# A mixture-of-experts layer whose second matrices move from token-major fp32 products to stationary float32r halves with 512 gated tokens moving

## The reference

```python
logits = x @ Wg + bg
topk_vals, topk_idx = top_k(logits, 2);  topk_w = softmax(topk_vals)
h = relu(einsum('bsd,edf->bsef', x, W1) + b1)
eo = einsum('bsef,efd->bsed', h, W2) + b2
mixed = sum(take(eo, topk_idx) * topk_w)
y = mixed + x
out = layernorm(gamma * (y - mu) * rsqrt(var + eps) + beta)
```

## Time and profile before

| | us |
|---|---|
| median of 3 runs (lowest, highest) | 232.52 (230.89, 234.33) |
| span of the profiled execution | 229.2 |
| its own time | not given apart; the runs' median is 3.3 above the span |
| PE busy | 215.3 (94%) |
| DVE busy | 181.3 (79%) |
| ACT busy | 142.5 (62%) |
| POOL busy | 111.6 (49%) |

### The profile page before, as it was taken

The page is one execution under the profiler, slowest core; times in us unless marked ns, Lnnn a source line. Parts: engine busy times, 40 slices in busy tenths (PEclk is TensorE's granted clock), DMA queues, the critical chain, the costliest instruction groups (busy, mean ns, idle before and its releaser), DMA issues.

```text
span 229.2 us, 7210 instructions
## 1 busy us (share of the span) xinstructions
PE 215.3 (94%) x2724; PEld 184.4 (80%) x2724; DVE 181.3 (79%) x622; ACT 142.5 (62%) x248; POOL 111.6 (49%) x219
## 2 busy tenths in 40 slices
PE   8989899999999989999999999999999999999970
PEld 7766677778777667778887999789988999889970
DVE  0589998999899899776755779897798868875885
ACT  2488899999999995674489300991029610596112
POOL 5089889999889995513630400252002600040484
PEclk9999999999999999999999999999999999999996
DMA  5951534765569941000000000001000100001001
GB/s 149 286 124 34 106 61 51 171 133 119 138 125 156 156 90 19 14 3 1 3 0 0 3 0 1 0 3 46 4 0 0 46 3 1 0 4 46 1 16 34
DMA packets 32455, 12.32 MB, mean 54 GB/s; under 512 B 19907, under 2 KB 32291, under 8 KB 32419
## 3 DMA queue, kind: packets, MB, share of 16 engines
q1 hardware_dynamic: 31554, 11.48, 24.5%
q10 hardware_dynamic: 864, 0.36, 0.6%
HBM read 6.33 MB, written 1.05 MB: 32 GB/s over the span
## 4 chain that ended last, share of the span: by engine, by line
PE 81%; DVE 6%; DMA 5%; ACT 3%; issue 2%; SPq 1%; DVEq 0%; ACTq 0%
PE bank L1326 13%; PE scoreT_pair L1326 12%; PE score_pair L1298 11%; PE scoreT_pair L1298 8%; PE bank L1042 6%; PE bank L1046 5%; DMA qT_all<-mT 5%; PE bank L965 4%; PE scoreT_pair L997 4%; PE bank L1003 3%; PE score_pair L981 3%; PE scoreT_pair L945 2%; PE bank L1059 2%; ACT early L737 2%; PE bank L940 1%
## 5 line engine op out<-in xcount | busy, mean ns | idle before, releaser
L1383 DVE TENSOR_REDUCE rowmax<-score_pair 128x8 f32<-128x1024 f32 x32 | 39.0, 1218 | 3.3 <-PE score_pair L981 2.0
L608 POOL TENSOR_TENSOR ve<-mv,table 128x4 f32<-128x4 f32 (+1 forms) x12 | 3.3, 277 | 78.1 <-DVE mv L1743 60.2
L737 ACT ACTIVATE early<-scoreT_pair 128x1024 f32<-128x1024 f32 x32 | 32.9, 1027 | 6.0 <-PE scoreT_pair L997 5.9
L1326 PE MATMUL bank<-w,early 128*128 128x128 f32 x256 | 30.1, 276 | 0.0
L1326 PE MATMUL scoreT_pair<-w,early 128*128 128x128 f32 x256 | 29.9, 275 | 0.0
L1326 PEld LDWEIGHTS bank<-w,early 128*128 128x128 f32 x256 | 29.5, 192 | 0.3
L1326 PEld LDWEIGHTS scoreT_pair<-w,early 128*128 128x128 f32 x256 | 29.2, 192 | 0.0
L1298 PE MATMUL score_pair<-x2T_part,w_part 128*128 128x512 f32 x108 | 28.4, 397 | 0.0
L880 ACT ACTIVATE early<-score_pair,b 128x512 f32<-128x512 f32 x38 | 26.0, 691 | 3.2 <-PE score_pair L1298 2.6
L1042 PE MATMUL bank<-early,v_pad 128*32 128x128 f32 x512 | 26.5, 279 | 0.4 <-DVE attnT L1399 0.3
L1046 PE MATMUL bank<-early,head_ones 128*32 128x128 f32 x512 | 25.8, 273 | 0.0
(11 more groups left out here) (229 smaller groups left out, 474.0 us busy)
## 6 DMA issues: line engine op xcount, KB each, us to landing
w<-in_w SPq DMA_DIRECT2D x8, 256.0 KB, 3.8
x_ext<-in_x SPq DMA_DIRECT2D x4, 256.0 KB, 5.4
qT_all<-mT SPq DMA_DIRECT2D x32, 32.0 KB, 2.3
early<-in_xT SPq DMA_DIRECT2D x3, 256.0 KB, 4.5
early<-in_ctxT SPq DMA_DIRECT2D x3, 256.0 KB, 5.1
out<-qkv_all SPq DMA_DIRECT2D x3, 256.0 KB, 2.3
table<-in_tables SPq DMA_DIRECT2D x1, 321.0 KB
qT_all<-stack SPq DMA_TRANSPOSE x13, 3.4
```

Source lines behind the costliest of these rows:

```text
L737: act.activation(prob[n % 2][:, 2 * u:2 * u + 2, :, :], scoreT_pair[:, :].rearrange("p (i j s) -> p i j s", i=2, j=QUAD), ACT.Exp, scale=S ...
L1326: mm = pe.matmul(expert_bank[k % 4][:, e4 * D:(e4 + 1) * D], hT[:, f, n * P:(n + 1) * P], w2[:, f, :], start=(c == 0), stop=(c == CH - 1))
L1383: dve.tensor_reduce(rowmax[:, H // 2 * u:H // 2 * (u + 1)], score_pair[:, :].rearrange("p (r t) -> p r t", t=S), AX_X, ALU.max).then_inc(s ...
```

## The change

1. **The second layer by feature.** For all but six (group, expert) pairs, `second(k)` on PE holds a 128 x 128 piece of w2 stationary and moves 512 tokens. w2 and the activations are split into float32r parts: w2_high x high, w2_low x high, w2_high x low, three matmuls of 512 columns a chunk. All chunks of a group add up in one bank (`yT_bank`), feature-major.
2. **The gate goes in ahead of the product.** DVE's `gated` takes the bank of the first layer: max(h, -b1) times the gate, in one instruction of 512 columns. (The relu leaves out +b1, which the b2 product makes up: b1 through w2 is added to b2 for each expert, by 16 matmuls, `turn_b1`, that take the place of idle ones, and by `shift_b2` on DVE.) ACT's `highs` rounds the result to float32r, POOL's `low` (for indices 2 and 3 of a group DVE's) subtracts for the low part. Buffers: 3 gated, 5 high, 4 low. `second` runs four chunks behind `hidden` (LAG).
3. **The gate as rows.** To multiply by token along the free axis, the gate must lie across all partitions: gates are transposed on PE, copied by ACT (`gate_rows`), written to DRAM and read back from there, spread over 128 partitions, 256 KB for each expert and group, all on the SP queue (`spread_gates`).
4. **The way back.** `keep_yT` on ACT copies the bank, `y_back` on PE transposes it in four pieces, `y_add` on DVE adds it to `acc`, one group late (in g3 at once).
5. **By token as before** stay experts 0 to 3 of g0, and 6 and 7 of g3.
6. **Other moves.** The first layer's banks are three in rotation instead of four. `pre_rows` and `post_results` go from DVE to ACT. The work of the next and of the last group is laid between the `gated` instructions on DVE. w2 is split by ACT and POOL in the correlation; POOL's `spread_b1` (a memset of 1536 columns and 17 small instructions) stands ahead of the inverse deviation of row tile 14.

```diff
+BY_TOKEN = ((0, 1, 2, 3), (), (), (6, 7))
+LAG = 4
+N_GATED, N_HIGH, N_LOW = 3, 5, 4
+LOW_ON_DVE = (2, 3)
...
         def hidden_bank(g, c):
-            return later_bank[c] if g else bank[c % 4]
+            return bank[(NCH * g + c) % 3]
+        yT_bank = (bank[4], bank[3], bank[4], bank[3])
...
+            def spread_gates(g):
+                wait_later(sp, "gate_rows_ready", g + 1)
+                sp.dma_start(gate_dram[g].rearrange("n e t -> (n e) t"), gate_rows[:, :]).then_inc(s["gate_kept"], 16)
+                wait_later(sp, "gate_kept", 16 * (g + 1))
+                for e in range(E):
+                    if e in BY_TOKEN[g]:
+                        continue
...
+                    sp.dma_start(gate_wide[e].rearrange("p (n t) -> p n t", n=GT), gate_dram[g, :, e, :].partition_broadcast(P))\
+                        .then_inc(s_gate[e][0], 16)
...
+            def low(g, i):
...
+                pool.tensor_tensor(low_in[k % N_LOW], gated_in[k % N_GATED][:, :], high_in[k % N_HIGH][:, :].bitcast(F32), ALU.subtract)\
+                    .then_inc(s["low_pool"], 1)
...
             def body(g):
-                hidden(g, 0, NCH)
+                highs(g, 0, 2)
+                rows(g + 1)
+                highs(g, 2, 4)
                 pre(g + 1)
+                highs(g, 4, 5)
+                keep_yT(g - 1)
+                highs(g, 5, 8)
                 exp_gap(g + 1)
+                highs(g, 8, 12)
                 gateT_copy(g + 1)
+                highs(g, 12, 15)
+                results(g - 1)
+                highs(g, 15, 16)
...
+                for i, (w, x) in enumerate(((w2_high, high_in[k % N_HIGH][:, :]), (w2_low, high_in[k % N_HIGH][:, :]), (w2_high, low_in[k % N_LOW]))):
+                    if i == 2:
+                        wait_low(pe, k)
+                    mm = pe.matmul(yT_bank[g][:, :], w[:, c, :], x, start=(k == first and i == 0), stop=(k == last and i == 2),
+                                   skip_group_check=True)
...
+            def layers(g, first, end):
+                for c in range(first, end):
+                    hidden(g, c, c + 1)
+                    second(gated_no(g, c) - LAG)
...
+            layers(3, 6, 12)
+            for c in range(12, NCH):
+                hidden(3, c, c + 1)
+                second(gated_before(G) - LAG + c - 12)
+            experts(3, 0)
+            experts(3, 1)
+            y_back(3)
+            experts(3, 2)
+            experts(3, 3)
...
+                    dve.scalar_tensor_tensor(gated_in[k % N_GATED][:, :], hidden_bank(g, c)[:, :], b1_neg[:, c:c + 1], gate_wide[e], ALU.max, ALU.mult)\
+                        .then_inc(s["gated"], 1)
```

More of the change, by code:

```diff
@@ new lines, in layers, with body @@
+            def layers(g, first, end):
+                for c in range(first, end):
+                    hidden(g, c, c + 1)
+                    second(gated_no(g, c) - LAG)
+            def body(g):
+                layers(g, 0, 1)
+                b2_mix(g)
+                layers(g, 1, 4)
+                x2_transpose(g + 1)
+                layers(g, 4, 6)
+                logits(g + 1)
+                y_back(g - 1)
+                layers(g, 6, 12)
+                gate_transpose(g + 1)
+                layers(g, 12, NCH)
@@ L1743, in gather, with sums_statistics, post_rows @@
                 dve.bn_aggr(mv3[:, n, :], st3[:, n, :]).then_inc(s["y3_aggr"], 1)
-            def post_sums(g, call, tiles=ALL):
-                numbers = range(tiles.start, tiles.stop)
-                for n in numbers:
+            def sums_statistics(g):
+                wait_later(dve, "y_added", g + 1)
+                statistics(lambda n: acc[:, g, n, :], st3, "y3_stats", mv3, "y3_aggr", g)
+            def post_rows(g):
+                for n in range(GT):
                     dve.wait_ge(s["y3_aggr"], GT * g + n + 1)
```

640 lines of the change are left out of this document (468 added, 172 removed).

## The result

The changed kernel takes 279.12 us (276.12 to 279.88, four runs) against 231.94 (230.89 to 234.33) for the kernel before in the same comparison: 1.200 times as long, 95% interval 1.194 to 1.207. The forecast said slower, but 244.5 us, and its range ended at 255. Of the 47.2 us that came, 12 were foreseen. The profiled execution has a span of 277.8 us, 48.6 above that of before. (Each run's time is some 2 us above its own span.

A forecast was written before the change was run, and what follows sets the result against it. PE alone was taken to bound the experts, POOL's chain the end. Span 227.3 plus 10.9 of waits plus 3.0 for the port gave 241.2, 12.0 above 229.2; 232.5 + 12.0 = 244.5 us, range 232 to 255.

The forecast's parts named there:

- my sum: Whole kernel: span 227.3 + 10.9 of PE's waits + 3.0 for the shared port = 241.2, 12.0 above 229.2.
- Part 1, PE's work: PE in g0 to g3: 11.1 us less from 52 chunks by feature, transposes added, net 8.9 us less.
- Part 2, the end: POOL's chain after g3: starts 1.2 us earlier, runs 1.0 shorter, `spread_b1` adds 0.3; span 227.3 if PE never waits.
- Part 3, what PE now waits for: g0 to g3: PE waits for DVE, gates and x2 rows, as three engines are nearly full; 10.9 us.
- Gates for g1: Start of g1: gate rows' write and spread read in series delay `gated`, 1.3 us (0 to 4).
- the end of g3: PE's waits at the end of the last group, 0.5 us.
- Part 4, POOL against DVE: g0 to g3: DVE instructions with two SBUF operands are held until POOL's ends, 3.0 us (0 to 12).
- My bounds for this part: Shared port: nothing where POOL happens to wait for DVE, up to 1.27 us for each place; 0 to 12 in all.
- The rival: Shared port costs much more: about 15 places lose half of POOL's 1.27 and more, 9 us, time 250; chance 0.12.
- what was to show it right: g1 25 to 28 us, PE waiting for `gated`, pairs 1.36, g0 ending on DVE, gates' DMA wait, POOL near 225, held DVE.
- POOL's start: End: POOL starts on the last group's tile 0 near 225, the last result 12.2 us after.
- what was to show it wrong: POOL on tile 0 before 216, `second` matmuls not 0.227, or PE waiting most for ACT or the DMA queue.

The follow-up runs named there:

- experiment 2: Changed kernel with each POOL low replaced by a same-size subtraction on constant tensors that nothing waits for, low part left out of the result: 275.96 us.
- experiment 1: Changed kernel without POOL's low subtractions; PE's third matmul moves the high part instead, except in the two chunks a group that DVE splits: 255.2 us.
- experiment 8: Changed kernel without POOL's lows, with spread gates read early from g0's rows and ACT's result rows and DVE's means moved later in the last group: 247.72 us.
- experiment 4: Kernel before, with POOL running one unused 512-column subtraction for each chunk of g1 and g2: 245.97 us, 1.055 times the kernel before.
- experiment 3: Changed kernel with each of POOL's low subtractions split into two of 256 columns: 273.31 us.
- experiment 5: Changed kernel with 18 (g1) and 26 (g2) extra small matmuls into a free bank where PE waited: 277.20 us.

## Why the prediction was wrong

The sign and its reason were right: an 8.9 us cut of PE's work is worth almost nothing, since the end is POOL's chain and the engines around PE were to become late. The size was off by 35 us. The steps from run to run share it out (medians, each good to about 2 us):

- *Lock by the lows*, experiment 2 less 1: 20.8 us, of which up to 2.8 may be waits in POOL's queue.
- *Waits for the lows*, the changed kernel less experiment 2: 3.1.
- *Gates and the order at the end*, experiment 1 less 8: 7.5 (3.1 and 4.1 alone, in the kernel with lows).
- *Experiment 8 over the kernel before*: 15.9, of which 7.7 were in my sum (12.0 less 3.0 for the port and 1.3 for the gates), 2.3 are the chunk pair and up to 4.4 the lock in g0 and ahead of it.

That the four add up to 47.3 for the 47.2 measured proves nothing, since each begins where the one ahead ends. What can be tested is inside them: the 19.6 us of longer instructions beside the 20.8, the 7.2 of two separate runs beside the 7.5, and 14.4 named of the 15.9. Some 1.5 us stay open.

By the steps of the prediction:

**Part 1, PE's work:** right in kind. Where the two layers alternate, a float32r matmul takes 0.233, not 0.227. The earlier trace rows has 1.39 and 1.36 for six matmuls, and I took the lower one as the rate for all 342.

**Part 2, the end:** right: 12.2 us from POOL's start to the last result, measured 12.2. The front: I gave `spread_b1` 0.3 us. It costs nothing; but from the last softmax reciprocal to the first layer's first whole chunk it is 17.39 us (101.53 to 118.92) where it was 16.06 (99.07 to 115.13), in experiments 1 and 8 17.4 and in experiment 4, whose front is the old one, 16.06. The 1.33 us are x2's first two rows, 1.93 instead of 0.60, held beside POOL's additions of the cross bias (114.19 to 116.69), which now come behind w2's low half. That is a part of the lock that no low causes.

**Part 3, what PE waits for, 10.9 us:** in experiment 8, where only these are left, it is 27.6 us from the transposes for g2's x2 (153.67) to those for g3's (181.25), beside 27.2 in the sum (23.9 + 2.3 + 1.0). Two items were too small. Gates for g1, 1.3 (0 to 4): the read took 5.4 us in g1 (5.9 in the median of 26, 4.5 to 7.2), not the 3.8 of the earlier trace rows. Such a row of 256 KB, of a large load, is not the price of 128 partitions fed from four rows. And "the end of g3: 0.5", where two orders of instructions (ACT's result rows ahead of the last high part, DVE's means ahead of the maxima) cost 4: I read the order of the loop's body and not of the tail that is written out behind it.

**Part 4, POOL against DVE, 3.0 us [0 to 12]:** the step that failed. The mechanism was named, its row was found and the price of one hold (up to 1.27) was right. Both factors were wrong: together they gave 3.0 us, where the runs show 20.8. *How many:* "12 places that PE waits behind". In fact nearly every DVE instruction with all its operands in SBUF can be held, the statistics left out, also those of 4 columns and those with one tensor operand; a group has some 20. (The cast of the gates kept its 0.195 in the changed kernel, but beside a half of experiment 3 it took 0.66 at 172.49 and again at 208.78. The result rows in experiment 4 are held too.) *How much:* "a quarter of a us". But POOL works for 22 to 24 of a group's 36 us, so an instruction meets a low more often than not, and loses half of 1.3 and more; measured on the forms, 0.44 for z (787 - 346), 0.55 for nm, 0.76 for gap (930 - 166), but 0.13 to 0.54 for the other steps of the routing. A sum of this kind comes near: POOL's busy share (23 of 38 us, 0.6) times half of 1.3 is 0.4 us an instruction; 20 of them in each of three groups' worth (g1, g2, the halves of g0 and g3) make 24 us, an estimate; beside the lows alone DVE's instructions are 19.3 us longer (experiment 1). The 38 us are known only now, though: with the 25 to 28 of my forecast the same sum gives 31 to 35. My bounds for this part didn't hold together either: 12 places at up to 1.27 are 15 us and not 12, and the range of the whole took in only 9. The rival had "about 15 places" and 9 us, and was too small for the same reason.

**Not in the prediction: PE's clock.** It falls after the longer waits (0.60 and 0.55 over 160 to 168, behind a stretch from 156 to 164 in which PE was busy for 4.5 us), to 0.91 over g1 and g2. With it held, experiment 5 is 1.9 us shorter, within the spread, since DVE is the bound; in experiment 4, where PE is, 4.6 us or more came with 7.7 us of waits.

Of what was to show it right: the first gated tokens of g1 did wait for the spread gates' DMA (3.94 us), and DVE instructions beside a low are longer than their kin. The window of g1 (38.5 against 25 to 28) and POOL's start (263 against 225) were wrong, mostly by the lock; without lows, in experiment 8, POOL starts at 230.4. Of what was to show it wrong, one thing came: the matmuls of `second` take 0.233.

## What to carry to other kernels

Before work goes to an idle POOL, count the instructions of DVE that read and write only SBUF and multiply by POOL's busy share to be and by half of POOL's instruction. That estimates a cost of DVE's, whatever the two compute (an estimate of 24 us here with the share as measured, where the instructions beside the lows were 19.3 longer). Here it made the idle engine as dear as the full one. What remedies there are: an operand in PSUM for the DVE instructions in the heaviest stretch (-7.6 us for one edit), shorter POOL instructions where DVE's come singly (-5.8). And where PE was the bound, a wait of 4.1 us came with 2.3 more behind it, so slack has to be read ahead of the one thing that PE waits for, not as a sum over the group.

## What was not expected of the hardware

- POOL's power of four columns doesn't hold DVE: two of the four yn, with two SBUF inputs, run from 183.6 to 184.2 beside it (183.58 to 184.60, in the timeline above), 1.24 us for four. In g2 the four take 1.23 us beside it (220.19, the power from 220.77). By the rule that the prediction went by they would have been held to its end. POOL's subtractions and its memset do: beside the memset of 1.38 us one row of x1 took 1.03 us instead of 0.34.
- Executions of one kernel differ in their first 12 us. In the changed kernel's profile three small fp32 matmuls (six records) took 1.63 us and the next three 1.18, where they took 0.91 and 0.91 before; its first softmax reciprocal started at 29.24 us, that of before at 27.42, and in the other profiles it is either 26.7 to 27.4 or 28.9 to 29.2. By the last one the two are 2.46 us apart (101.53 and 99.07), in a stretch with the same instructions. So 2.5 of the 48.6 us between the spans are not the change's, and a difference of 2 us between two kernels' times is no more than this:

```profile
7.04 1.63 PE L1186 MATMUL scoreT_pair<-mean_w 128*128 128x128 f32 x6
10.05 1.18 PE L1186 MATMUL scoreT_pair<-mean_w 128*128 128x128 f32 x6
```
